# One graph-attention layer on one core: edges sorted in lots of four and nine blocks, uneven fetches, one square per group

## The reference

```python
x = h @ W                                  # 256 -> 64
el = x @ Wl.T ; er = x @ Wr.T              # 4 heads
e = exp(leaky_relu(el[src] + er[dst], 0.2))
w = e / segment_sum(e, src)[src]
out = segment_sum(w * x[dst], src)         # per head, 6250 x 4 x 64
out = elu(out + b)
```

## Time and profile before

| what | us |
|---|---|
| runs (3) | 2986.27, 2997.49, 2994.30; median 2994.3 |
| the profiled execution | 2988.45, span 2986.6 |
| POOL busy | 1825.2 (61%) |
| DVE, PE, ACT busy | 2065.1 (69%), 1888.2 (63%), 1868.2 (63%) |
| mean granted TensorE clock | 0.593 of full |

### The profile page before, as it was taken

How to read it: one execution, slowest core, us unless ns; L and a number is a source line. 1 busy time by engine, 2 the same in 40 slices (tenths; PEclk the granted TensorE clock), 3 DMA queues, 4 the chain that set the end, 5 groups by cost and what they waited for, 6 DMA issues and landing times.

```text
span 2986.6 us, 48066 instructions
## 1 busy us (share of the span) xinstructions
PE 1888.2 (63%) x8550; PEld 1584.1 (53%) x8551; DVE 2065.1 (69%) x4596; ACT 1868.2 (63%) x6576; POOL 1825.2 (61%) x1826
## 2 busy tenths in 40 slices
PE   1763365157676667888887665655656562478993
PEld 0331332046566666777776555555555552367772
DVE  8988688866677667888887666665655656844453
ACT  1443343177678778999998666666666664654541
POOL 0004788877777777437777777777777750444453
PEclk8786677555555555555555555555555555589996
DMA  9011211133323332111111111111111115234664
GB/s 322 8 12 33 52 41 30 45 100 89 89 74 89 89 87 77 53 35 28 28 29 28 28 29 28 28 28 28 29 28 29 28 22 144 85 116 155 191 200 135
DMA packets 159838, 206.71 MB, mean 69 GB/s; under 512 B 47107, under 2 KB 117051, under 8 KB 159490
## 3 DMA queue, kind: packets, MB, share of 16 engines
q0 software_dynamic: 60992, 82.75, 12.8%
q1 hardware_dynamic: 91408, 115.05, 11.8%
q10 hardware_dynamic: 7346, 7.92, 0.9%
HBM read 124.08 MB, written 74.97 MB: 67 GB/s over the span
## 4 chain that ended last, share of the span: by engine, by line
POOL 52%; issue 18%; PE 12%; DVE 8%; ACT 7%; DMA 2%; ACTq 1%; SPq 0%; POOLq 0%; DVEq 0%
POOL arena L1665 51%; PE ps L1310 4%; PE ps L1326 3%; DVE arena L699 2%; DVE arena L700 2%; ACT arena L1496 1%; PE ps L1131 1%; ACT arena L1485 1%; PE ps L1318 1%; PE ps L1302 1%; ACT arena L1474 1%; ACT ps L1475 1%; PE ps L1234 1%; POOL arena L1688 1%; PE ps L1262 1%
## 5 line engine op out<-in xcount | busy, mean ns | idle before, releaser
L1665 POOL DMA_INDIRECT arena<-gather_table,arena x1612 | 1620.9, 1006 | 821.2 <-issue 488.0
L1234 PE MATMUL ps<-arena 128*128 x4784 | 1097.4, 421 | 387.8 <-DVE big L888 382.4
L1234 PEld LDWEIGHTS ps<-arena 128*128 128x128 f32 x4784 | 1042.8, 330 | 454.2 <-issue 453.9
L864 DVE TENSOR_TENSOR ps<-ps,arena 128x512 f32<-128x512 f32 x598 | 388.0, 694 | 388.6 <-ACT arena L1491 323.6
L1496 ACT ACTIVATE arena<-lane,arena 128x32 f32<-128x32 f32 x2392 | 536.4, 311 | 0.0
L1485 ACT ACTIVATE arena<-arena 128x2 f32 x1196 | 254.3, 286 | 418.4 <-SPq L1774 251.5
L877 DVE TENSOR_TENSOR arena<-ps,arena 128x1024 f32<-128x1024 f32 x299 | 365.9, 1224 | 117.7 <-ACT ps L1475 117.6
L872 DVE TENSOR_TENSOR ps<-ps,arena 128x1024 f32<-128x1024 f32 x299 | 367.6, 1229 | 36.3 <-ACT arena L1496 35.9
L1224 PE MATMUL ps<-el,pick_w 48*128 x1196 | 204.6, 294 | 221.2 <-issue 166.6
L1474 ACT ACTIVATE arena<-ps 128x1024 f32<-128x1024 f32 x299 | 302.4, 1011 | 62.1 <-issue 61.4
L1475 ACT ACTIVATE ps<-ps 128x1024 f32<-128x1024 f32 x299 | 302.7, 1012 | 0.0
(11 more groups left out here) (292 smaller groups left out, 1898.5 us busy)
## 6 DMA issues: line engine op xcount, KB each, us to landing
arena<-gather_table,arena POOLq DMA_INDIRECT x1612, 2.4
staged_rows<-arena SPq DMA_DIRECT2D x40, 552.0 KB, 2.8
arena<-staged_rows SPq DMA_DIRECT2D x40, 552.0 KB, 5.1
arena<-slot_rows SPq DMA_DIRECT2D x119, 128.0 KB, 2.2
expert_rows<-arena SPq DMA_DIRECT2D x119, 128.0 KB, 2.7
slot_rows<-ends_w SPq DMA_DIRECT2D x2, 4480.0 KB, 25.5
arena<-big SPq DMA_DIRECT2D x112, 56.9 KB
slot_rows<-ends_w SPq DMA_DIRECT2D x1, 6272.0 KB, 33.1
```

The lines of the kernel that those rows point to most:

```text
L864: ins = dve.tensor_tensor(z5[:, :, c, :, :], row, bcast(er[:, :, c, :], 3, WN), ALU.add)
L1234: ins = pe.matmul(ps[:, 6 + u % 2, i * AW:i * AW + AW], share_w[u % 4][:, (i * GT + c) * P:(i * GT + c + 1) * P], gat[:, bass.ds(place["ag ...
L1665: pool.indirect_dma_start(rows, None, table_d, bass.IndirectOffsetOnAxis(ap=dst_x[:, t:t + 1], axis=0)).then_inc(s_gat[p % LAND], 16)
```

## The change

Three edits, one in each stage.

1. The lots: lot 0 has four blocks and 16 levels, lot 1 nine blocks and 18 levels, in the parts (0,4) and (4,9). Lot 0 takes PSUM bank 0 and lot 1 banks 1 to 3. `NPA` becomes 256, so lot 0 has 256 + 195 = 451 items and lot 1 550 + 195 = 745.
2. The fetches: `FETCH_AT` says in which of SP's turns stage n is fetched: turns 10 to 13 for the first four, then 14 + (n - 3) * 29 // 40, so that 36 fetches share turns 14 to 40 (before: one a turn, turns 14 to 49).
3. The square: DVE makes the distance of lane and place for all eight columns of a group in one tensor_tensor of 128 x 256 (`distances`), between `add_ers` and `put_away`; ACT then squares it in one activation of 128 x 256 instead of eight of 128 x 32. The place is now kept unscaled.

```diff
-    LOTS = ((0, 5, 17, ((0, 5),)), (5, NB - 5, 17, ((0, 4), (4, NB - 5))))
+    LOTS = ((0, 4, 16, ((0, 4),)), (4, NB - 4, 18, ((0, 4), (4, NB - 4))))
...
-    STAGE, STAGES, AHEAD = 8, 3, 10
+    STAGE, STAGES = 8, 3
...
+    FETCH_AT = [10 + n if n < 4 else 14 + (n - 3) * 29 // 40 for n in range(NST)]
...
-        turned = [ps[:, b:b + 2, :].rearrange("p a (b m) -> p (a b) m", m=P)[:, 0:LOTS[lot][1], :] for lot, b in enumerate((0, 2))]
+        turned = [ps[:, a:b, :].rearrange("p a (b m) -> p (a b) m", m=P)[:, 0:LOTS[lot][1], :] for lot, (a, b) in enumerate(((0, 1), (1, 4)))]
...
+            def distances(g, u):
+                par = u % 2
+                dve.wait_ge(s_loc, g + 1)
+                after(dve, s_zsub, g, 2)
+                dve.tensor_tensor(away[par], bcast(lane[:, 0:WN], 1, GS), bcast(loc[par][:, :], 2, WN), ALU.subtract).then_inc(s_dist, 1)
...
-                for i, (part, lag) in enumerate(((add_ers, 1), (put_away, 1), (weigh, 2))):
+                for i, (part, lag) in enumerate(((add_ers, 1), (distances, 0), (put_away, 1), (weigh, 2))):
...
+                after(act, s_dist, g, 2)
                 for i in range(GI):
                     ins = act.activation(loc[par][:, i * GT:i * GT + GT], src_f[:, bass.ds(place["tile", u][i], GT)], ACT.Identity,
-                                         bias=bases[:, sl(g * GI + i)], scale=-FAR)
+                                         bias=bases[:, sl(g * GI + i)])
...
-                act.wait_ge(s_loc, g + 1)
-                after(act, s_zsub, g, 2)
-                for j in range(GS):
-                    ins = act.activation(away[par][:, j, :], lane[:, 0:WN], ACT.Square, bias=loc[par][:, j:j + 1], scale=FAR)
-                ins.then_inc(s_away, 1)
+                act.wait_ge(s_dist, g + 1)
+                act.activation(away[par], away[par], ACT.Square, scale=FAR).then_inc(s_away, 1)
...
-            for n in range(NST + AHEAD):
+            for n in range(max(NST, FETCH_AT[-1] + 1)):
                 if n < NST:
                     spill(n)
                 if n == 3:
                     left_terms()
-                if n >= AHEAD:
-                    fetch(n - AHEAD)
+                for q in range(NST):
+                    if FETCH_AT[q] == n:
+                        fetch(q)
```

More of the change, by code:

```diff
@@ L401, in gps_layer @@
         s_loc = sem("s_loc")
+        s_dist = sem("s_dist")
         s_away = sem("s_away")
@@ L847, in _ @@
             step(dve.tensor_copy(wi, tab[:, 3, :]))
-            step(dve.tensor_scalar(window, window, float(WN) * FAR, None, ALU.mult), "tables")
+            step(dve.tensor_scalar(window, window, -float(WN), None, ALU.mult), "tables")
             dve.wait_ge(s_arow, T)
@@ L901, in group @@
                     if sums_:
-                        for q in ((0,), (1,), (2, 3))[i]:
+                        for q in ((0,), (), (1,), (2, 3))[i]:
                             add_up(g - 5, (u - 5) % UNROLL, q)
```

## The result

The changed kernel takes 3012.2 us (median of 4 runs, 3010.4 to 3014.4), the kernel before 2992.2 (4 runs): ratio 1.0068, interval 1.0046 to 1.0089. The forecast was 3020.

A forecast was written before the change was run, and what follows sets the result against it. The end was set by when pair 352 may start, plus 1134 us of gathers and 541 of stage D. Pair 352 at 1328, gathers 1135 and contention 13 end POOL 30 us later: 3018, put at 3020, range 2950 to 3055.

The forecast's parts named there:

- POOL's start: Lot 0's sort gets 37 us shorter, less 6 of longer waits: POOL starts some 31 us earlier, near 226.
- Lot 1: Lot 1's sort starts 31 us earlier but takes 55 more, so the consumer starts at 631, 24 us later.
- The square: DVE's new tensor_tensor adds 0.34 us a group: a turn of 20.13 us, 5.03 a group against 4.88.
- The fetches: SP's fetches, due each 14.5 us but free each 17.7, delay spills; POOL goes at 24.4 us a stage, not 20.
- Contention: Gathers meeting DVE's new instruction lose 0.07 us a group on average: 13 us over 181 groups, bounds 0 and 76.
- contention rival: Collisions of DVE and gathers repeat: 0.42 us lost per group, or DVE held 0.35 a group; 3070 us, chance 0.08.
- Stage D: The stage after POOL's gathers, 541 us, is unchanged.
- SP isn't late: Rival: the consumer gains what ACT lost, near 4.5 us a group; 2957 us, chance 0.24.
- PE's length: Rival: DVE's gap hides most of the new instruction and PE sets 4.75 us a group; 2987 us, chance 0.16.
- Lot 1 late: Rival: lot 1's blocks and half levels wait longer for PE and ACT, tables at 650; 3039 us, chance 0.08.
- third lots term: The items: pair 288 comes after 124 groups instead of 116, the extra 7.7 groups costing 38 us at 4.88.

The follow-up runs named there:

- nosquare: The changed kernel with ACT's eight squares per group restored and DVE's tensor_tensor removed: 2987.6 us, ratio 0.9986 to the kernel before.
- slope35: The changed kernel with the fetches' slope at 35 fortieths in place of 29: 2956.3 us, ratio 0.9878 to the kernel before.
- fetch31: The kernel before with uneven fetches alone, slope 31 fortieths: ratio 1.0017 beside a kernel before of 3690.8 us; run again, 0.9996 beside 3719.6.
- lots: The kernel before with the new lots alone: 3712.3 us, ratio 0.9998, beside a kernel before of 3714.4.
- base: The kernel before with only an edit in how register values are read, values unchanged: 3715.2 us, ratio 1.0001, beside a kernel before of 3714.4.

## Why the prediction was right

Slower was forecast for two reasons, a longer turn of DVE ahead of a fetch order that hangs on it, and stretched gathers. Both were shown. Step by step:

- *POOL's start.* 226 forecast, 222.3 measured.
- *Lot 1.* The working had it 24 us later; it ended at 568.0, 13.4 later than in the earlier trace rows, and ACT's first place came at 620.3, not 631. At 10.7 us this is the largest miss of a term. The count of 13 more plain steps was exact (122 instructions of 320 keys instead of 109), but lot 1 as a whole took 48 us more, not 55, and POOL started 4 earlier. Which of the smaller terms was too dear, no run splits.
- *The square.* Turn 20.13 forecast, 20.00 measured; ACT is off the bound and waits for DVE. The instruction adds 0.26 a group (4.56 against 4.30), not 0.34. It is not hidden by DVE's gap, which stays at 1.67. Undoing it gave 24.6 us, which the working had at 118 x 0.15 + 13 = 31.
- *The fetches.* The first late fetch was due to go at 665 and went at 653.8, which is the earlier start. POOL's slack was to be gone "within a few fetches"; its first wait for a spill of more than 0.3 us came at 902.5, fifteen fetches on. From there the spills come 24.45 us apart on average (24.4 forecast). 118.2 groups in 1237.90 - 620.32 - 16.3 = 601.3 us are 5.09 each, not 5.03: DVE's own 5.00 plus the seven long register loads, 12.1 us or 0.10 a group, which no term of the working has. This gave back 6.7 of the 10.7 us of the early start, so that the close hit at 1242 is two misses that partly cancel. Fetch of the last spill 1242 forecast, 1237.9 measured; pair 320 1248 and 1244.4; pair 352 1328 and 1324.3, with no wait of its own, as expected.
- *Contention.* 13 us forecast, 11.9 measured, and this is luck in the size. The working took L874 to meet the gathers at random: a third of 181 groups at 0.21 us. Behind pair 352 160 groups ran, and 105 gathers were stretched, by 0.115 on average. The loop does move in step with the gathers there, as the contention rival had it: ACT waits for gathers 137 times (354.4 us), and in 146 of the 160 groups a gather begins some 0.1 to 0.3 us behind L874. So it is hit twice as often and pays half as much.
- *Stage D.* Taken as unchanged; it was 2.7 us shorter. So the span was 3009.4, not 3017.

Of the rivals, "SP isn't late" fails on POOL's 112.8 us of waits for spills and DVE's turn, which it put at 18 us. "PE's length" falls with `nosquare`. "Lot 1 late" had the tables at 650; ACT's first place came at 620.3. The strong contention rival, 0.42 lost in each group, would have made the spacing about 1.33 (76 us over 907 gathers); it is 1.263.

What the prediction did not weigh enough is its own third lots term. Pair 288 stands at group 124, not 116, which alone is 8 x 5.00 = 40 us of consumer time; `slope35` shows that this, with the later start, is then what pair 352 waits for. By the same sum five and eight blocks with a fitting slope would reach pair 352 some 50 us earlier than `slope35`'s 1263 as far as the consumer goes, and POOL's own work, 1159.1 + 80, would be the bound at about 1240. That is argued, not shown: the run meant for it, `fetch31`, met the stalls twice. Equally open is what the lots do alone at 2992, and so how the 5 us of lots and fetches together divide.

## What to carry to other kernels

A queue that holds both a producer's stores and a consumer's loads makes the producer wait for the consumer. A load placed ahead of a store should be due only after the consumer, at its real pace, has freed its place; else it takes the producer's slack away. One constant of this schedule (29 or 35 fortieths) was worth 56 us, more than twice the square's 25. Where engines stand level within 4%, as here, work taken off the longest one and put on the next can make the loop longer: count the turn of each, register gaps included, before moving an instruction. And look for the wait that comes later before paying for an earlier start: POOL's 35 us were gone at its later waits, here and in `lots`.

## What the runs showed of the hardware

A gather is stretched when it starts just behind a DVE instruction that reads two SBUF operands. In the changed kernel, behind pair 352, 105 gathers took over 1.00 us, mean 1.059, where the others take 0.94. All 105 began 0.10 to 0.24 us after L874 did, and all ended 0.80 to 0.82 after it ended. In the kernel before and in `nosquare` not one gather behind pair 352 took over 1.00. In `slope35` it is 114 of mean 1.098, and the spacing is 1.270 us. It fits that gathers are stretched in the kernel before while it sorts, where DVE's minimum and maximum also read two SBUF operands: between 257 and 555 us 73 of 168 took over 1.00, mean of all 1.48, the longest 10.28; what held each of these was not traced. POOL and DVE of `slope35`:

```profile
1587.61 1.19 POOL L1672 DMA_INDIRECT arena<-gather_table,arena  x1 [0.30 <-issue]
```

```profile
1587.55 0.43 DVE L874 TENSOR_TENSOR arena<-lane,arena 128x256 f32<-128x256 f32 x1 [1.34 <-ACT arena L1495]
```

The gather begins 0.06 us after the subtraction, takes 0.25 longer than the others and ends 0.82 after it (1588.80 against 1587.98), as the gather of the earlier trace rows did under an instruction sixteen times as long. The excess, 105 x (1.059 - 0.944) = 12.1 us, is the lengthening of the gathers' time (11.9); in `slope35` 114 x 0.154 = 17.5, against 906 x (1.270 - 1.250) = 18. The Trainium skill (page "SBUF — State Buffer", sections "SBUF: two separate sides" and "Who interferes with whom") has whichever of the two started first hold the other for its whole length. The trace agrees for gathers held by DVE, and not the other way: L874 has a mean of 423 ns over 299, as long as the sort's instruction of this size, at most 494, and is nowhere held for a gather's 0.94.

In the kernel before and in `slope35` a register load of DVE takes 1.10 to 1.11 us (median of 75) and at most 1.36. In the changed kernel the longest took 2.97 and in `nosquare` 2.87: there SP, held by the consumer, issues seven spills at the very moment (within 0.02 and 0.14 us) at which DVE comes to its gap. All 14 such gaps are 3.1 to 3.5 us long instead of 1.67. What ties the load to the spill no run shows.

The stalls were not expected: in three of five sets of runs every kernel, the one before included, was 23 to 24% slower, with instructions of unchanged length coming late: by 1.2 us in the rows of `base` above, and by up to 4.1 at ACT's squares. What makes them was not found; it is not the granted clock, and it is not the chip alone, since the same chip gave 3714 in one set and 2992 in the next. Ratios compare a kernel only with the kernel before of the same set.
